# A graph layer on one core: VectorE's hand-written order changed, so that large additions from SBUF stand apart

## The chip, the core and the metric

One Trainium2 chip, one core of it. The metric is the device time of one launch, in microseconds. All data are fp32 at the kernel's border; x has 50,000 rows of 128, there are 25,000 edges.

## What is computed

The layer is a residual graph block. Every row of x is layer-normalised and cut at zero, the edges' attributes are summed per source node, a two-layer perceptron takes both, its result is normalised again, and both inputs are added back:

```python
h = maximum(layernorm(x), 0)                       # 50000 x 128
agg = segment_sum(edge_attr_128, src, 50000)       # 25000 edges, 128 wide
z = silu(concat([h, agg]) @ W1 + b1) @ W2 + b2     # 256 -> 256 -> 128
z = (z - mean(z)) * rsqrt(var(z) + 1e-5) * gamma + beta
out = x + (z + h)
```

## The kernel before, in words

The program is fully unrolled, and each engine's instructions stand in an order written out by hand, with semaphores between the engines. It has two stages. Up to about 125 us a first stage finds, for each of 392 tiles of 128 nodes, which edges belong to it and packs one edge per slot (`hot_tile`, `hot_slot`, `rank`; then `slot_edge` and `slot_node`). The change does not touch it, and only its end, the start of the second, is seen below.

The second stage runs over 49 blocks of 1,024 nodes (8 tiles of 128 each), and each block in two halves `c` of 4 tiles. The engines are several steps apart in it:

- SyncE loads X (512 KB a block, four blocks ahead) and stores R, the result, once both `result` operations of its block are done.
- POOL (GpSimd) fetches the edges' rows. For each tile it copies one column of `slot_edge` into `gather_rows` (line 418) and then issues one indirect DMA into G (line 430): 8 copies and 8 gathers a block, in turn. G has three buffers, so POOL can be up to three blocks ahead of TensorE.
- TensorE, per half: `turn_h` transposes H (line 595) into `za`; `sum_edges` (line 602) waits for the four gathers of that half and sums them there with the one-hot matrices HOT; `layer1` (lines 613, 614, 618) works on the half before; `layer2` (lines 626, 630) on the one before that. `turn_h` of a half needs `hi` and `lo` of the half before it to be taken out of `za`.
- ScalarE, per half: casts `za` to `hi` (lines 500, 502), squares of y for the second norm (515), `normalise` (493: H from X, with `shift` and `rstd`), and silu (508).
- VectorE, per block and in this order, in `step`: `split_low` of the second half (`lo<-za,hi`, line 870); a HOT matrix (861); `scale` of both halves (886: T from y, 4 operations each); `result` of both (896: R from T and R); `residual` (878: R from H and R); `split_low` of the next block's first half; then `powers` of a later block. `powers` is a chain of 13 small operations on 8 or 16 columns (lines 732 to 752) that gives both norms' `rstd` by Newton's steps. Each of the small ones waits for the one before it, and `link_small` puts another piece of work into that wait, by its place in the chain.

What VectorE's large operations read matters below. `R<-T,R`, `R<-H,R`, `R<-X,betas` and `HOT<-iota_node,slot_node` read two operands from SBUF, 512 columns each; there are two of each a block, eight in all. `lo<-za,hi` and `T<-y,rstd,gammas` read one from PSUM and one from SBUF; `stat<-X` (BN_STATS, line 697) reads one. In the text the eight are called **the eight additions**, though two of them compare.

Of the kernel before, what the change touches and what calls it, by code (L numbers as in the profile page):

```python
# [16 lines left out]
TILES = 8  # L17
# [72 lines left out]
def at_least(engine, semaphore, value):  # L90

    if value > 0:
        engine.wait_ge(semaphore, value)


def gnn_layer(nc, x, src, edge_attr, W1, b1, W2, b2, gamma, beta, out):
# [4 lines left out]
    NB = -(-nodes // BLOCK)  # L101
# [12 lines left out]
    with ExitStack() as ctx:  # L114
# [541 lines left out]
        def _(dve):  # L656
# [35 lines left out]
            def statistics(b, t):  # L692

                if t == 0:
                    dve.wait_ge(x_loaded[b.xj], b.x_lap(16, 16))
                    at_least(dve, powers_done, b.number(1, -1))
                done = nc.vector.bn_stats(stats[b.ring(2)][:, t, :], X[b.xj][:, t, :])  # L697
                if t == TILES - 1:
                    done.then_inc(bn_done, 1)

            SMALLS = 4 + 3 * NEWTON

            def powers(b):


# [3 lines left out]
                def link_small(instruction):  # L709

                    count[0] += 1
                    instruction.then_inc(small, 1)
                    place = count[0] - 1
                    if place == 0 and b.exists(NB) and not b.is_number(0):
                        one_hots(b, 0)
                    if 1 <= place <= TILES and b.plus(1).exists(NB):
                        statistics(b.plus(1), place - 1)
                    if b.plus(-2).exists(NB) and not b.is_number(0) and not b.is_number(1):
                        if place in (TILES + 1, TILES + 2):
                            x_plus_beta(b.plus(-2), place - TILES - 1)  # L720
                        if place == TILES + 3:
                            residual(b.plus(-2), 0)
                    dve.wait_ge(small, b.number(SMALLS, count[0]))

# [124 lines left out]
            def x_plus_beta(b, c):  # L849
                dve.wait_ge(x_loaded[b.xj], b.x_lap(16, 16))  # L850
                at_least(dve, stored[b.j], b.lap(16))
                s = slice(c * HALF, (c + 1) * HALF)
                nc.vector.tensor_tensor(out=R[b.j][:, s, :], in0=X[b.xj][:, s, :],
                                        in1=betas[:].unsqueeze(1).to_broadcast([P, HALF, D]),
                                        op=ALU.add).then_inc(xb_done, 1)
# [11 lines left out]
            def split_low(b, c):  # L867
                dve.wait_ge(hi_done, b.half(c, 1, 1))
                at_least(dve, pre_done, b.half(c, 2, -2))
                nc.vector.tensor_tensor(out=lo[c][:], in0=za[:], in1=hi[c][:].bitcast(F32),  # L870
                                        op=ALU.subtract).then_inc(lo_done, 1)

            def residual(b, c):

                dve.wait_ge(xb_done, b.half(c, 1, 1))
                dve.wait_ge(h0_done, b.half(c, 1, 1))
                s = slice(c * HALF, (c + 1) * HALF)
                nc.vector.tensor_tensor(out=R[b.j][:, s, :], in0=H0[b.j][:, s, :], in1=R[b.j][:, s, :],
                                        op=ALU.add).then_inc(r_done, 1)

            def scale(b, c):

                dve.wait_ge(powers_done, b.number(1, 1 + RING))
                for t in range(HALF):
                    n = TILES + c * HALF + t
                    done = nc.vector.scalar_tensor_tensor(  # L886
                        out=T[c][:, t, :], in0=y[2 * b.ring(2) + c][:, t * D:(t + 1) * D],
                        scalar=rstd[b.j][:, n:n + 1], in1=gammas[:], op0=ALU.mult, op1=ALU.mult)
                done.then_inc(t_done, 1)

            def result(b, c):

                dve.wait_ge(t_done, b.half(c, 1, 1))
                dve.wait_ge(r_done, b.half(c, 1, 1))
                s = slice(c * HALF, (c + 1) * HALF)
                nc.vector.tensor_tensor(out=R[b.j][:, s, :], in0=T[c][:], in1=R[b.j][:, s, :],
                                        op=ALU.add).then_inc(out_done, 1)
# [8 lines left out]
            def step(b):  # L906
                split_low(b, 1)
                if b.plus(1).exists(NB):
                    one_hots(b.plus(1), 1)
                if b.is_number(0):  # L910
                    slot_tables(FIRST_BLOCKS * TILES, NT)
                elif not b.is_number(1):
                    for c in range(2):
                        scale(b.plus(-2), c)
                    for c in range(2):
                        result(b.plus(-2), c)
                if not b.is_number(0):
                    residual(b.plus(-1), 1)
                if b.plus(1).exists(NB):
                    split_low(b.plus(1), 0)  # L920
                powers(b.plus(2))

            run_blocks(step)
# [32 lines left out]
```

## Time and profile before

| what | value |
|---|---|
| median of 3 runs | 801.94 us (800.46 to 802.87) |
| the profiled execution: its own time | 803.43 us |
| the profiled execution: its span | 801.9 us, 15882 instructions |
| TensorE busy, weight loads busy | 733.6 us (91%), 592.4 us (74%) |
| VectorE busy | 732.1 us (91%) |
| ScalarE busy | 587.0 us (73%) |
| POOL busy | 601.1 us (75%) |
| mean granted TensorE clock | 0.974 |

The page divides the span into 40 slices; from the sixth the second stage runs, and there TensorE and VectorE are busy over 90% of nearly every slice, and POOL about as much. Busy shares so high on three engines do not say which of them sets the pace; the chain of waits and the timelines do.

### The profile page before, as it was taken

The page shows a single profiled execution, that of the slowest core. Times are in us where ns is not written, and L with a number is a line of the kernel's source. Part 1 is how long each engine was busy: PE and PEld are TensorE (multiplying, and loading weights), DVE is VectorE, ACT ScalarE, POOL GpSimd, SP SyncE. Part 2 cuts the span into 40 slices and gives each one's busy share as a digit, 9 for nine tenths or more (in the row PEclk, how much of TensorE's full clock was granted, in tenths as well). Part 3 has the DMA queues.
Part 4 walks back from the last instruction along what each step waited for, and adds up shares of the span by engine and source line. Part 5 has one row for each costly group of instructions (what it writes and reads, how often), then busy time and mean ns, then how long its engine had stood idle before and what let it go on. Part 6 is the DMA issues. An engine that isn't in the chain of part 4 may idle for free.

```text
span 801.9 us, 15882 instructions
## 1 busy us (share of the span) xinstructions
PE 733.6 (91%) x4567; PEld 592.4 (74%) x4616; DVE 732.1 (91%) x2494; ACT 587.0 (73%) x1927; POOL 601.1 (75%) x831
## 2 busy tenths in 40 slices
PE   4999993989999999999999999999999999989990
PEld 1455542878888888888888888888888888878880
DVE  6999995879999999999999999999999999989994
ACT  4999982767777777777777777777777777757860
POOL 4600006889998999889989998999989998989920
PEclk9999995999999999999999999999999999999996
DMA  5000000122323333332323232323233332321211
GB/s 191 2 1 2 1 0 17 48 74 75 124 90 110 98 103 99 102 120 80 126 74 126 74 125 74 127 78 121 91 107 100 102 107 93 126 66 51 71 61 48
DMA packets 28159, 65.86 MB, mean 82 GB/s; under 512 B 8379, under 2 KB 9934, under 8 KB 28070
## 3 DMA queue, kind: packets, MB, share of 16 engines
q1 hardware_dynamic: 15526, 51.90, 18.6%
q0 software_dynamic: 12544, 12.93, 6.5%
q8 instruction: 37, 0.61, 0.3%
q14 instruction: 52, 0.43, 0.2%
HBM read 51.98 MB, written 25.60 MB: 97 GB/s over the span
## 4 chain that ended last, share of the span: by engine, by line
POOL 66%; ACT 10%; issue 8%; PE 8%; DVE 5%; DMA 1%; SPq 0%; POOLq 0%; DVEq 0%
POOL G L430 50%; POOL gather_rows L418 16%; ACT junk_rank L472 10%; PE y L630 2%; PE za L602 1%; PE pre L613 1%; PE pre L614 1%; DVE hot_tile L768 1%; PE pre L618 1%; DVE hot_slot L790 1%; DVE T L886 1%; DMA srci<-in_src_dram 1%; DMA G<-in_edge_attr_dram,gather_rows 1%; PE za L595 0%; DVE is_slot L781 0%
## 5 line engine op out<-in xcount | busy, mean ns | idle before, releaser
L430 POOL DMA_INDIRECT G<-in_edge_attr_dram,gather_rows x392 | 440.6, 1124 | 63.4 <-POOL gather_rows L418 48.2
L418 POOL COPY gather_rows<-slot_edge 128x1 uint32<-128x1 uint32 x392 | 138.5, 354 | 92.0 <-DVE slot_edge L842 89.6
L630 PE MATMUL y<-w2c,S 128*128 128x128 f32 x1568 | 190.9, 275 | 3.3
L630 PEld LDWEIGHTS y<-w2c,S 128*128 128x128 f32 x1568 | 191.5, 192 | 2.5
L493 ACT ACTIVATE H<-X,shift,rstd 128x128 f32<-128x128 f32 x392 | 162.4, 508 | 7.7 <-DVE shift L752 7.6
L613 PE MATMUL pre<-hi,w1h 128*128 128x512 f32 x392 | 164.8, 420 | 0.4 <-issue 0.4
L870 DVE TENSOR_TENSOR lo<-za,hi 128x1024 fp32r<-128x1024 f32 x98 | 119.8, 1222 | 46.5 <-ACT hi L502 42.3
L614 PE MATMUL pre<-hi,w1l 128*128 128x512 f32 x392 | 156.1, 398 | 0.0
L500 ACT CAST hi<-za 128x512 fp32r<-128x512 f32 x98 | 57.4, 586 | 123.5 <-PE za L595 113.6
L602 PE MATMUL za<-HOT,G 128*128 128x128 f32 x784 | 114.4, 290 | 18.4 <-issue 10.1
L508 ACT ACTIVATE S<-pre,b1c 128x512 f32<-128x512 f32 x196 | 125.3, 697 | 5.0 <-remote 2.1
L602 PEld LDWEIGHTS za<-HOT,G 128*128 128x128 f32 x784 | 97.1, 195 | 37.4 <-DMA G<-in_edge_attr_dram,gather_rows 31.5
L618 PE MATMUL pre<-lo,w1h 128*128 128x512 f32 x392 | 124.0, 397 | 0.0
L697 DVE BATCH_NORM_STATS2 stat<-X 128x6 f32<-128x128 f32 x392 | 109.0, 284 | 0.0
L515 ACT ACTIVATE junk_sq<-y 128x128 bf16<-128x128 f32 x392 | 103.7, 286 | 3.5 <-PE y L630 3.5
L886 DVE SCALAR_TENSOR_TENSOR T<-y,rstd,gammas 128x128 f32<-128x128 f32 x392 | 105.6, 341 | 0.0
L502 ACT CAST hi<-za 128x512 fp32r<-128x512 f32 x98 | 57.6, 588 | 42.4 <-PE za L602 25.0
L618 PEld LDWEIGHTS pre<-lo,w1h 128*128 128x128 f32 x392 | 74.4, 190 | 18.1
L613 PEld LDWEIGHTS pre<-hi,w1h 128*128 128x128 f32 x392 | 75.0, 191 | 14.3 <-issue 0.8
L515 ACT ACTIVATION_READ_ACCUMULATOR junk_sq<-y 128x1 f32 x392 | 85.0, 217 | 0.0
L614 PEld LDWEIGHTS pre<-hi,w1l 128*128 128x128 f32 x392 | 75.0, 191 | 13.4
L595 PE MATMUL za<-ident,H 128*128 128x128 f32 x392 | 59.8, 276 | 13.4 <-ACT H L493 9.0
(123 smaller groups left out, 1047.3 us busy)
## 6 DMA issues: line engine op xcount, KB each, us to landing
X<-in_x_dram SPq DMA_DIRECT2D x48, 512.0 KB
out_dram<-R SPq DMA_DIRECT2D x48, 512.0 KB
G<-in_edge_attr_dram,gather_rows POOLq DMA_INDIRECT x392
X<-in_x_dram SPq DMA_DIRECT2D x1, 424.0 KB
out_dram<-R SPq DMA_DIRECT2D x2, 212.0 KB
w1f<-in_L_gnn_W_dram SPq DMA_DIRECT2D x1, 256.0 KB, 3.3
w2f<-in_L_gnn_W_dram SPq DMA_DIRECT2D x1, 128.0 KB, 2.6
srci<-in_src_dram SPq DMA_DIRECT2D x1, 97.2 KB
```

What stands on the lines that cost most here:

```text
L418: nc.gpsimd.tensor_copy(gather_rows[b.xj][:, t:t + 1], slot_edge[:, bass.ds(b.number(TILES, t), 1)]).then_inc(row_named, 1)
L430: nc.gpsimd.indirect_dma_start(G[b.j][:, t, :], None, source, bass.IndirectOffsetOnAxis(ap=gather_rows[b.xj][:, t:t + 1], axis=0), bounds_ ...
L493: done = nc.scalar.activation(H0[b.j][:, t, :], X[b.xj][:, t, :], ACT.Relu, bias=shift[b.j][:, t:t + 1], scale=rstd[b.j][:, t:t + 1])
L508: nc.scalar.activation(S[c][:, m, :], pre[m][:], ACT.Silu, bias=b1c[:, m:m + 1]).then_inc(silu_done, 1)
L515: done = nc.scalar.activation(junk_sq[:, p, c * HALF + t, :], y[2 * p + c][:, t * D:(t + 1) * D], ACT.Square, scale=float(D) ** -0.5, accu ...
L602: done = nc.tensor.matmul(za[:, 1, t * P:(t + 1) * P], G[b.j][:, c * HALF + t, :], HOT[b.j][:, c * HALF + t, :], start=True, stop=True)
L613: nc.tensor.matmul(pre[m][:], w1h[:, k, cols], hi[c][:, k, :], start=(k == 0), stop=False)
L614: nc.tensor.matmul(pre[m][:], w1l[:, k, cols], hi[c][:, k, :], start=False, stop=False)
L618: done = nc.tensor.matmul(pre[m][:], w1h[:, k, cols], lo[c][:, k, :], start=False, stop=(k == 1))
L630: done = nc.tensor.matmul(place[:, t * D:(t + 1) * D], S[c][:, m, t * P:(t + 1) * P], w2c[:, m, :], start=False, stop=(t == HALF - 1 and m ...
L870: nc.vector.tensor_tensor(out=lo[c][:], in0=za[:], in1=hi[c][:].bitcast(F32), op=ALU.subtract).then_inc(lo_done, 1)
L886: done = nc.vector.scalar_tensor_tensor(out=T[c][:, t, :], in0=y[2 * b.ring(2) + c][:, t * D:(t + 1) * D], scalar=rstd[b.j][:, n:n + 1], i ...
```

## The change

VectorE's order in the second stage is written anew; no operation is added, removed or resized, and no other engine's order changes. In `powers` the fillers of the small chain are placed otherwise: BN_STATS at places 0, 2, 3, 5, 6, 8, 9 and 11, the HOT matrix at place 1, the two `x_plus_beta` at 4 and 7, the `residual` at 10 (before: HOT at 0, BN_STATS at 1 to 8, `x_plus_beta` at 9 and 10, `residual` at 11). In `step` the `residual` moves between the two `scale`, the first `result` follows the second `scale`, and `split_low` of the next half goes ahead of the second `result`.

```diff
+            STATISTICS_PLACES = (0, 2, 3, 5, 6, 8, 9, 11)
...
-                    if place == 0 and b.exists(NB) and not b.is_number(0):
+                    if place == 1 and b.exists(NB) and not b.is_number(0):
                         one_hots(b, 0)
-                    if 1 <= place <= TILES and b.plus(1).exists(NB):
-                        statistics(b.plus(1), place - 1)
-                    if b.plus(-2).exists(NB) and not b.is_number(0) and not b.is_number(1):
-                        if place in (TILES + 1, TILES + 2):
-                            x_plus_beta(b.plus(-2), place - TILES - 1)
-                        if place == TILES + 3:
+                    if place in STATISTICS_PLACES and b.plus(1).exists(NB):
+                        statistics(b.plus(1), STATISTICS_PLACES.index(place))
+                    if b.plus(-2).exists(NB):
+                        if place in (4, 7):
+                            x_plus_beta(b.plus(-2), (4, 7).index(place))
+                        if place == 10:
                             residual(b.plus(-2), 0)
...
-                elif not b.is_number(1):
-                    for c in range(2):
-                        scale(b.plus(-2), c)
-                    for c in range(2):
-                        result(b.plus(-2), c)
+                two_back = not b.is_number(0) and not b.is_number(1)
+                if two_back:
+                    scale(b.plus(-2), 0)
                 if not b.is_number(0):
                     residual(b.plus(-1), 1)
+                if two_back:
+                    scale(b.plus(-2), 1)
+                    result(b.plus(-2), 0)
                 if b.plus(1).exists(NB):
                     split_low(b.plus(1), 0)
+                if two_back:
+                    result(b.plus(-2), 1)
                 powers(b.plus(2))
```

VectorE, the first part of a step, before (T is the scaled result of the perceptron, R the sum that will be stored):

```order
L870 TENSOR_TENSOR lo1<-za,hi1 128x1024
L861 TENSOR_TENSOR HOT1<-iota_node,slot_node 128x512
L886 SCALAR_TENSOR_TENSOR T0<-y0,rstd1,gammas 128x128 x4
L886 SCALAR_TENSOR_TENSOR T1<-y1,rstd1,gammas 128x128 x4
L896 TENSOR_TENSOR R1<-T0,R1 128x512
L896 TENSOR_TENSOR R1<-T1,R1 128x512
L878 TENSOR_TENSOR R2<-H02,R2 128x512
L870 TENSOR_TENSOR lo0<-za,hi0 128x1024
L729 TENSOR_TENSOR msum<-stat0 128x8
```

The same part in the change; every line number behind the new table is higher by two:

```order
L872 TENSOR_TENSOR lo1<-za,hi1 128x1024
L863 TENSOR_TENSOR HOT1<-iota_node,slot_node 128x512
L888 SCALAR_TENSOR_TENSOR T0<-y0,rstd1,gammas 128x128 x4
L880 TENSOR_TENSOR R2<-H02,R2 128x512
L888 SCALAR_TENSOR_TENSOR T1<-y1,rstd1,gammas 128x128 x4
L898 TENSOR_TENSOR R1<-T0,R1 128x512
L872 TENSOR_TENSOR lo0<-za,hi0 128x1024
L898 TENSOR_TENSOR R1<-T1,R1 128x512
L731 TENSOR_TENSOR msum<-stat0 128x8
```

Three additions stood in a row; now a group of `T` or a `lo` stands between any two of them, and `lo0` has moved ahead of one.

VectorE, the end of `powers`, before (`guess_sq`, `guess_off` and `guess` are the small chain, 16 columns):

```order
L697 BN_STATS stat0<-X4 128x6
L750 SCALAR_TENSOR_TENSOR guess0<-guess_off,guess1 128x16
L853 TENSOR_TENSOR R1<-X1,betas 128x512
L747 SCALAR_TENSOR_TENSOR guess_sq<-guess0 128x16
L853 TENSOR_TENSOR R1<-X1,betas 128x512
L749 TENSOR_TENSOR guess_off<-guess_sq,var 128x16
L878 TENSOR_TENSOR R1<-H01,R1 128x512
L750 SCALAR_TENSOR_TENSOR rstd0<-guess_off,guess0 128x16
```

The same end in the change, from the second of the two `R<-X,betas`:

```order
L855 TENSOR_TENSOR R1<-X1,betas 128x512
L751 TENSOR_TENSOR guess_off<-guess_sq,var 128x16
L697 BN_STATS stat0<-X4 128x6
L752 SCALAR_TENSOR_TENSOR guess0<-guess_off,guess1 128x16
L697 BN_STATS stat0<-X4 128x6
L749 SCALAR_TENSOR_TENSOR guess_sq<-guess0 128x16
L880 TENSOR_TENSOR R1<-H01,R1 128x512
L751 TENSOR_TENSOR guess_off<-guess_sq,var 128x16
L697 BN_STATS stat0<-X4 128x6
L752 SCALAR_TENSOR_TENSOR rstd0<-guess_off,guess0 128x16
```

Between two additions there was one small operation; now there are three and two BN_STATS. The first `R<-X,betas` stands as far ahead of the second. A small operation of two SBUF operands still stands right before and right behind each of these additions.

## Rows read from the trace of the kernel before

**Rows 1.** The page: shares of the chain that ended last, by line
```profile
POOL G L430 50%; POOL gather_rows L418 16%; ACT junk_rank L472 10%; PE y L630 2%; PE za L602 1%; PE pre L613 1%; PE pre L614 1%; DVE hot_tile L768 1%; PE pre L618 1%; DVE hot_slot L790 1%; DVE T L886 1%; DMA srci<-in_src_dram 1%; DMA G<-in_edge_attr_dram,gather_rows 1%; PE za L595 0%; DVE is_slot L781 0%
```

**Rows 2.** Groups of POOL, 206 to 710 us: xcount | busy us, mean ns | idle before
```profile
L430 POOL DMA_INDIRECT G<-in_edge_attr_dram,gather_rows x307 | 341.8, 1113 | 48.6 <-POOL gather_rows L418 39.9 <-issue 8.7
L418 POOL COPY gather_rows<-slot_edge 128x1 uint32<-128x1 uint32 x307 | 112.0, 365 | 1.9
```

**Rows 3.** Lines L418 and L430, whole span: duration ns min/median/max
```profile
L418 POOL COPY gather_rows<-slot_edge x392: 185/199/1185, 123.6 to 765.1; 128x1 uint32<-128x1 uint32 x196
...
L430 POOL DMA_INDIRECT G<-in_edge_attr_dram,gather_rows x392: 997/1030/2731, 125.9 to 767.5; - x196
```

**Rows 4.** Timeline of TensorE: start us, length us, form, idle before
```profile
205.63 1.16 PE L602 MATMUL za<-HOT,G 128*128 128x128 f32 x8
...
710.13 1.16 PE L602 MATMUL za<-HOT,G 128*128 128x128 f32 x8
...
733.52 1.06 PE L602 MATMUL za<-HOT,G 128*128 128x128 f32 x8
...
739.67 1.06 PE L602 MATMUL za<-HOT,G 128*128 128x128 f32 x8
...
770.48 1.16 PE L602 MATMUL za<-HOT,G 128*128 128x128 f32 x8
```

**Rows 5.** Timeline of VectorE, parts of 421 to 444 us
```profile
421.30 1.28 DVE L896 TENSOR_TENSOR R<-T,R 128x512 f32<-128x512 f32 x2
422.50 0.69 DVE L878 TENSOR_TENSOR R<-H,R 128x512 f32<-128x512 f32 x1
...
430.58 1.22 DVE L870 TENSOR_TENSOR lo<-za,hi 128x1024 fp32r<-128x1024 f32 x1
431.72 0.68 DVE L861 TENSOR_TENSOR HOT<-iota_node,slot_node 128x512 f32<-128x512 f32 x1
432.32 2.15 DVE L886 SCALAR_TENSOR_TENSOR T<-y,rstd,gammas 128x128 f32<-128x128 f32 x8
434.39 1.28 DVE L896 TENSOR_TENSOR R<-T,R 128x512 f32<-128x512 f32 x2
...
436.97 1.22 DVE L870 TENSOR_TENSOR lo<-za,hi 128x1024 fp32r<-128x1024 f32 x1 [0.70 <-ACT hi L502]
...
439.85 0.16 DVE L747 SCALAR_TENSOR_TENSOR guess_sq<-guess 128x16 f32<-128x16 f32 x1
439.92 0.28 DVE L697 BATCH_NORM_STATS2 stat<-X 128x6 f32<-128x128 f32 x1
440.13 0.15 DVE L749 TENSOR_TENSOR guess_off<-guess_sq,var 128x16 f32<-128x16 f32 x1
...
443.66 1.22 DVE L870 TENSOR_TENSOR lo<-za,hi 128x1024 fp32r<-128x1024 f32 x1
```

**Rows 6.** Timeline of POOL, 420 to 424 us
```profile
420.54 0.20 POOL L418 COPY gather_rows<-slot_edge 128x1 uint32<-128x1 uint32 x1
420.89 1.03 POOL L430 DMA_INDIRECT G<-in_edge_attr_dram,gather_rows  x1 [0.15 <-issue]
421.93 0.69 POOL L418 COPY gather_rows<-slot_edge 128x1 uint32<-128x1 uint32 x1
422.78 1.30 POOL L430 DMA_INDIRECT G<-in_edge_attr_dram,gather_rows  x1 [0.16 <-POOL gather_rows L418]
```

**Rows 7.** Timeline of POOL and VectorE, 725 to 728 us
```profile
725.88 1.28 DVE L896 TENSOR_TENSOR R<-T,R 128x512 f32<-128x512 f32 x2
725.93 2.73 POOL L430 DMA_INDIRECT G<-in_edge_attr_dram,gather_rows  x1 [0.16 <-issue]
```

**Rows 8.** Chain of waits in order of time, near 714 us
```profile
714.23 5.26 DMA G<-in_edge_attr_dram,gather_rows
```

**Rows 9.** Timelines of ScalarE and TensorE, 431 to 435 us
```profile
431.43 1.66 ACT L493 ACTIVATE H<-X,shift,rstd 128x128 f32<-128x128 f32 x4
...
434.53 0.60 PE L595 MATMUL za<-ident,H 128*128 128x128 f32 x4
```

## The prediction

> **What bounds the kernel now.** I read the chain of waits first, because three engines look full. It runs through POOL's gathers for 50% of the span and through its copies for 16% [rows 1]: in the second stage POOL works without a pause and the rest follows. TensorE confirms it. Its `sum_edges` starts 77 halves apart at 205.63 and 710.13 us, so 6.55 us a half and 13.10 a block; later, once it is not waiting for gathers, the same work takes 6.15 us from 733.52 to 739.67, 12.30 a block [rows 4]. So 0.80 us a block is TensorE waiting for POOL.
>
> POOL is slow because of VectorE. A copy takes 0.199 us at the median and a gather 1.030, but the means from 206 to 710 us are 0.365 and 1.113 [rows 2, 3]. The excess is 0.166 + 0.083 = 0.249 us a tile, 1.99 a block of 8 tiles. The idle time is (48.6 + 1.9)/307 = 0.16 us a tile, its normal spacing before a gather. Unhindered, a tile costs 0.20 + 0.16 + 1.03 = 1.39 us and a block 11.11; 11.11 + 1.99 = 13.10, the pace seen.
>
> Where the excess arises is seen with two timelines side by side. Two `R<-T,R` start at 421.30 and 421.90 and `R<-H,R` at 422.50, 0.60 us each [rows 5]. The copy of 421.93, just behind the second one's start, ends at 422.62, 0.12 after that addition's end; the gather of 422.78 falls into the third and ends at 424.08, 0.98 after its end at 423.10, so 0.27 late [rows 6]. The copy of 420.54 takes 0.20: VectorE reaches its additions only at 421.30 [rows 5, 6]. So POOL needs a door that is shut while VectorE reads two SBUF operands. **The rule I use**: a copy that starts inside an addition (or up to about 0.07 before it) ends 0.12 after it; a gather that starts inside ends 0.98 after it.
>
> Does adjacency itself matter? The copy of 421.93 got through between two additions that touch. The gather of 725.93, 0.05 after the first of three, was kept out by all three: 725.88 + 3 x 0.60 + 0.98 = 728.66, its end [rows 7]. So the door can stay shut over a row of additions, but rarely did.
>
> **The change part by part.** Nothing is added or removed, on any engine or queue, so what VectorE executes costs 0. The order moves each addition; three things follow.
>
> *1. POOL's waits.* Take the first `lo` of the step as 0. From the spacings in [rows 5] (`lo` 1.14, an addition 0.60, four `T` 1.04, a BN_STATS 0.20, a small one 0.08) the additions now begin at 1.14 (HOT), 2.78, 4.42, then 6.16 (behind `lo0`), 7.3, 8.6, 9.8 and 11.05 (the last four inside `powers`), and the next step at about 12.3. Lay POOL's cycle (copy at 0, gather at 0.35, next copy at 1.39) beside it, beginning with a copy at 6.3 in the addition of 6.16 to 6.76:
> copy 6.3 held 0.43, gather 7.1 free; copy 8.1 and gather 8.4 free, between 7.9 and 8.6; copy 9.5 free; gather 9.8 meets an addition's start and is held 0.56; copy 11.4 held 0.2; gather 12.0, copy 13.0 and gather 13.4 free; copy 14.4 free; gather 14.7 free; copy 15.8 and gather 16.1 free; copy 17.2 held 0.04; gather 17.6 free, and the next copy is at 18.6, which is 6.3 again one step later. The waits sum to 1.23 us. If the gather of 9.8 wins its race, it is held 0.44 one addition later and the copies of the next step 0.11 and 0.25: again 1.23. POOL would need 11.11 + 1.23 = 12.34 a block.
> The reason in words: the additions used to stand in a row of three and, in `powers`, three with 0.08 between them, and a POOL instruction let in behind one fell into the next; now they are 1.1 to 1.7 us apart, close to POOL's own 1.39, and a released copy leads POOL through the gaps. Bounds: above all zero waits, 11.11, where TensorE decides; below, 8 additions at 0.43 or more, 14.6.
>
> *2. Who is next.* TensorE needs 12.30 [rows 4]. VectorE takes 443.66 - 430.58 = 13.08 with 0.70 idle before `lo0`, so 12.38 of its own [rows 5]. POOL at 12.34, TensorE at 12.30 and VectorE at 12.38 nearly tie; I take 12.38. Over the 38.5 blocks that POOL now paces this is 38.5 x (13.10 - 12.38) = 27.7 us less. The other blocks already ran at TensorE's pace; I add 0.4 us for VectorE there.
>
> *3. The late gather.* One gather issued at 714.23 landed only after 5.26 us [rows 8]. The nine halves from 710.13 to 770.48 took 60.35 us instead of 9 x 6.15 = 55.35 [rows 4]: 5.0 lost, since POOL had no lead. With POOL no longer the bound, it keeps whatever lead it has early on, G has three buffers, and such a landing is covered. I count the 5.0 as gained; if POOL's lead is used up, it stays.
>
> *4. `lo0` ahead of a result.* One 0.60 addition moves from before `lo0` to behind it. The stretch from `lo0` to the next `lo1` grows from 6.69 to 7.29 [rows 5] against halves of 6.15, so `lo1` and the `shift` right before it come up to 1.1 us after `hi`. Covers: ScalarE's `normalise` begins at 431.43, 0.85 after `lo1` at 430.58, and needs only the `shift` before it, so it slips by about 0.3; its H is ready at 433.09 and TensorE's transposes of it begin at 434.53, 1.44 later [rows 5, 9], of which halves shorter by 0.4 leave enough. `lo1`, ready at 431.8, has 2.7 to spare for them. Cost 0; without the cover, 0.3 us a block, 12 in all. The second `T` group and the second `result` come one addition later, and a store with them; that R buffer is needed again a block later: 0.
>
> **Sum.** 803.4 - 27.7 + 0.4 - 5.0 = 771.1 for an execution like the profiled one. That one lies 1.5 above the median of 801.9, so **770 us** against the median.
>
> **The rivals.**
> *A, the forecast* (0.60): 12.3 to 12.4 a block, 765 to 776.
> *B, POOL still paces, but less* (0.20): the walk above has close races (at 8.4, 9.8 and 13.4). Losing one and settling in another pattern leaves 1.4 to 1.8 of waiting, 12.5 to 12.9 a block: 38.5 x 0.2 to 0.6 = 8 to 23 us less, 779 to 794. For it: a difference of 0.05 us decides each race.
> *C, no change* (0.08): each of the eight additions still shuts the door for 0.60, and what counts is their total, 4.8 us a block before and after. POOL's cycle of 1.39 meeting an addition at any phase waits 0.42 on average where the next to come is a gather (0.35 of 1.39) and 0.17 where it is a copy, together 0.23: 8 x 0.23 = 1.9, nearly the 1.99 seen. Then 13.1 stays, 802. The Trainium skill, SBUF — State Buffer, section on SBUF's two separate sides, states this: a VectorE instruction with two SBUF inputs and a GpSimd instruction that reads SBUF exclude each other, each for its whole instruction, so adjacency alone should be free. By that rule the copy of 421.93 agrees and the gather of 725.93 does not. Against C speaks that phases are not random: POOL's waits repeat from block to block, since a wait ends on VectorE's beat.
> *D, slower* (0.12): with additions 1.2 to 1.3 apart, POOL may lock in just behind the start of each. Copies there wait 0.43 to 0.5 and gathers up to 0.56. Five such waits are 2.4 us, 13.5 a block: 38.5 x 0.4 = 15 more, 817. It decides from 2.0 us of waiting a block on. The last blocks speak for it a little: there, with TensorE at its own pace, one wait grew to 1.70 [rows 7].
>
> **How the numbers follow.** Faster by over 0.3% (about what a measurement of this kernel can tell) is A and B: 0.80. Same is C: 0.08. Slower is D: 0.12. The range for 8 in 10 holds A and nearly all of B, and 5 us below the forecast for smaller losses: 764 to 793.
>
> **What would show it.** In the changed profile POOL's mean copy should fall from 0.365 to about 0.29 and its mean gather from 1.113 to 1.10, together 1.2 to 1.3 us of excess a block; `sum_edges` should start 6.15 to 6.2 us apart; POOL's share of the chain should fall far below its 66%, TensorE and VectorE taking it; the wait of TensorE's weight loads for G should nearly vanish, and VectorE's wait before `lo0` shrink from 0.70 to below 0.2. If POOL's excess stays near 2.0, point 1 is wrong and C holds; if it falls to 1.2 while the blocks stay above 12.6, point 2 or 4 is.

## The result and the profile after

The changed kernel takes 768.83 us at the median of four runs (767.88 to 771.23), the kernel before 802.4 beside it; the ratio is 0.9589, 95% interval 0.9558 to 0.9619. It is 4.1% faster. The forecast was 770, and the profiled execution, for which the prediction's sum gave 771.1 before the last step to the median, took 771.23.

The page of the kernel after: spans and busy times, and the chain that ended last by engine and by line.

```profile
span 769.7 us, 15882 instructions
...
PE 717.4 (93%) x4567; PEld 590.0 (77%) x4616; DVE 733.0 (95%) x2494; ACT 586.2 (76%) x1927; POOL 563.7 (73%) x831
...
DVE 63%; issue 14%; ACT 10%; POOL 5%; PE 3%; DMA 2%; DVEq 0%; SPq 0%; POOLq 0%
DVE T L888 12%; ACT junk_rank L472 10%; DVE lo L872 8%; DVE HOT L863 7%; DVE R L855 7%; DVE stat L697 6%; POOL G L430 4%; DVE R L898 4%; DVE R L880 4%; DVE guess_sq L749 3%; DVE guess_off L751 2%; DVE guess L752 1%; POOL gather_rows L418 1%; DVE hot_tile L770 1%; DVE rstd L752 1%
```

POOL's 66% of the chain [rows 1] have become 5%, and the bulk of it now runs along VectorE's own instructions, line after line. VectorE's busy time is what it was, 733.0 against 732.1 us; it is the 32 us of span around it that have gone. A share of the chain tells where one chain ran, though, and not how much time an engine has to spare: see e7 below.

The groups of POOL of the kernel after, 206 to 710 us (columns as in [rows 2]):

```profile
L430 POOL DMA_INDIRECT G<-in_edge_attr_dram,gather_rows x325 | 357.8, 1101 | 51.9 <-POOL gather_rows L418 51.9
L418 POOL COPY gather_rows<-slot_edge 128x1 uint32<-128x1 uint32 x325 | 93.2, 287 | 2.0
```

In the same 504 us POOL now issues 325 gathers instead of 307. A gather is 0.071 us above its median of before, a copy 0.088: 0.159 a tile, 1.27 a block, where it was 1.99.

TensorE's timeline of the kernel after (start us, length us, form):

```profile
204.37 1.06 PE L602 MATMUL za<-HOT,G 128*128 128x128 f32 x8
...
682.39 1.06 PE L602 MATMUL za<-HOT,G 128*128 128x128 f32 x8
688.53 1.06 PE L602 MATMUL za<-HOT,G 128*128 128x128 f32 x8
694.78 1.06 PE L602 MATMUL za<-HOT,G 128*128 128x128 f32 x8
...
738.05 1.06 PE L602 MATMUL za<-HOT,G 128*128 128x128 f32 x8
```

The first two rows are the same halves, 77 apart, as the first two of [rows 4]. They give the account of the whole difference, in executions of 801.9 and 769.7 us of span:

| stretch | before | after | difference |
|---|---|---|---|
| up to `sum_edges` of half 11 | 205.63 | 204.37 | -1.26 |
| the next 77 halves | 504.50 | 478.02 | -26.48 |
| the last nine halves | 60.35 | 55.66 | -4.69 |
| from the last `sum_edges` to the end | 31.42 | 31.65 | +0.23 |
| sum | | | -32.2 |

A block takes 12.42 us instead of 13.10, and its two halves are unequal, 6.14 and 6.25 us in the rows above.

### The profile page after: what moved, and what is told of

Read it like the earlier page. It is cut to its first block, busy times and chain, and to the rows that moved or that the text cites. A ratio compares the mean times of both kernels' runs of the same rounds, so it can differ in the third digit from the quotient of the medians.

```text
span 769.7 us, 15882 instructions
## 1 busy us (share of the span) xinstructions
PE 717.4 (93%) x4567; PEld 590.0 (77%) x4616; DVE 733.0 (95%) x2494; ACT 586.2 (76%) x1927; POOL 563.7 (73%) x831
## 4 chain that ended last, share of the span: by engine, by line
DVE 63%; issue 14%; ACT 10%; POOL 5%; PE 3%; DMA 2%; DVEq 0%; SPq 0%; POOLq 0%
DVE T L888 12%; ACT junk_rank L472 10%; DVE lo L872 8%; DVE HOT L863 7%; DVE R L855 7%; DVE stat L697 6%; POOL G L430 4%; DVE R L898 4%; DVE R L880 4%; DVE guess_sq L749 3%; DVE guess_off L751 2%; DVE guess L752 1%; POOL gather_rows L418 1%; DVE hot_tile L770 1%; DVE rstd L752 1%
## 5 line engine op out<-in xcount | busy, mean ns | idle before, releaser
L430 POOL DMA_INDIRECT G<-in_edge_attr_dram,gather_rows x392 | 430.4, 1098 | 63.8 <-POOL gather_rows L418 62.2
L418 POOL COPY gather_rows<-slot_edge 128x1 uint32<-128x1 uint32 x392 | 111.3, 284 | 92.0 <-DVE slot_edge L844 89.6
L872 DVE TENSOR_TENSOR lo<-za,hi 128x1024 fp32r<-128x1024 f32 x98 | 119.3, 1218 | 13.3 <-ACT hi L502 13.2
L508 ACT ACTIVATE S<-pre,b1c 128x512 f32<-128x512 f32 x196 | 123.6, 684 | 1.8 <-PE pre L618 1.7
L602 PE MATMUL za<-HOT,G 128*128 128x128 f32 x784 | 106.9, 280 | 5.0 <-DMA G<-in_edge_attr_dram,gather_rows 5.0
L888 DVE SCALAR_TENSOR_TENSOR T<-y,rstd,gammas 128x128 f32<-128x128 f32 x392 | 109.6, 341 | 0.0
L614 PEld LDWEIGHTS pre<-hi,w1l 128*128 128x128 f32 x392 | 74.4, 190 | 13.3
L595 PE MATMUL za<-ident,H 128*128 128x128 f32 x392 | 62.0, 281 | 11.0 <-ACT H L493 9.0
```

The source lines that it names most:

```text
L430: nc.gpsimd.indirect_dma_start(G[b.j][:, t, :], None, source, bass.IndirectOffsetOnAxis(ap=gather_rows[b.xj][:, t:t + 1], axis=0), bounds_ ...
L508: nc.scalar.activation(S[c][:, m, :], pre[m][:], ACT.Silu, bias=b1c[:, m:m + 1]).then_inc(silu_done, 1)
L602: done = nc.tensor.matmul(za[:, 1, t * P:(t + 1) * P], G[b.j][:, c * HALF + t, :], HOT[b.j][:, c * HALF + t, :], start=True, stop=True)
L614: nc.tensor.matmul(pre[m][:], w1l[:, k, cols], hi[c][:, k, :], start=False, stop=False)
L888: done = nc.vector.scalar_tensor_tensor(out=T[c][:, t, :], in0=y[2 * b.ring(2) + c][:, t * D:(t + 1) * D], scalar=rstd[b.j][:, n:n + 1], i ...
```

## What the eight additions do to POOL now

VectorE's timeline of the kernel after, the additions and `lo` of one step:

```profile
424.07 1.21 DVE L872 TENSOR_TENSOR lo<-za,hi 128x1024 fp32r<-128x1024 f32 x1
425.20 0.67 DVE L898 TENSOR_TENSOR R<-T,R 128x512 f32<-128x512 f32 x1
426.34 0.68 DVE L863 TENSOR_TENSOR HOT<-iota_node,slot_node 128x512 f32<-128x512 f32 x1
427.64 0.68 DVE L855 TENSOR_TENSOR R<-X,betas 128x512 f32<-128x512 f32 x1
...
428.88 0.68 DVE L855 TENSOR_TENSOR R<-X,betas 128x512 f32<-128x512 f32 x1
...
430.23 0.68 DVE L880 TENSOR_TENSOR R<-H,R 128x512 f32<-128x512 f32 x1
...
436.53 1.21 DVE L872 TENSOR_TENSOR lo<-za,hi 128x1024 fp32r<-128x1024 f32 x1
```

POOL's timeline of the kernel after, the same microseconds:

```profile
423.87 0.32 POOL L418 COPY gather_rows<-slot_edge 128x1 uint32<-128x1 uint32 x1
...
425.38 0.58 POOL L418 COPY gather_rows<-slot_edge 128x1 uint32<-128x1 uint32 x1
...
428.53 0.20 POOL L418 COPY gather_rows<-slot_edge 128x1 uint32<-128x1 uint32 x1
428.89 1.61 POOL L430 DMA_INDIRECT G<-in_edge_attr_dram,gather_rows  x1 [0.16 <-POOL gather_rows L418]
430.51 0.46 POOL L418 COPY gather_rows<-slot_edge 128x1 uint32<-128x1 uint32 x1
```

These four are all that POOL waits for in a step. The walk in the prediction put them at the same additions: the copy in the `R<-T,R` behind `lo0` (0.43 forecast, 0.58 - 0.20 = 0.38 here), the gather that meets the start of the second `R<-X,betas` (0.56; 1.61 - 1.03 = 0.58), the copy at `R<-H,R` (0.2; 0.26) and the one at the next step's `R<-T,R` (0.04; 0.12). One block later the large ones stand at the same places: copies of 0.57 at 437.85 and 0.46 at 442.97, the gather of 1.61 at 441.36.

## The experiments

Their texts call the theory of the prediction's first point "phases": only where a POOL instruction's start falls decides what it waits. The rival is "adjacency": what costs is that additions touch.

### The two halves of the change

**e1_step_only** keeps the new `step` and has the old table in `powers`:

```diff
-                    if place in STATISTICS_PLACES and b.plus(1).exists(NB):
-                        statistics(b.plus(1), STATISTICS_PLACES.index(place))
+                    if 1 <= place <= TILES and b.plus(1).exists(NB):
+                        statistics(b.plus(1), place - 1)
...
-                        if place in (4, 7):
+                        if place in (TILES + 1, TILES + 2):
```

> Only the part of the change in `step` (residual between the two scales, lo0 ahead of the second result); `powers` keeps the fillers of before. Theory 1, phases: what counts is where POOL's cycle of 1.39 us meets the eight additions. Laid beside this order, POOL's copies and gathers run into about five of the eight, some 2.3 us of waiting a block, so 13.3 to 13.5 us a block and about 812 us: slower than the kernel before, although half of the adjacent additions are apart. Theory 2, adjacency: what counts is that additions no longer touch; the three in a row are apart now, those of `powers` not, so about half of the gain, 783 to 788. Theory 3, POOL's total wait is set by the total time of the additions: no change, 802.

Measured: 821.75 us (817.26 to 824.01), ratio 1.0243 [1.0195, 1.0291]. **Half of the change alone makes the kernel slower than it was**, though fewer additions touch than before. Its groups of POOL, 206 to 710 us:

```profile
L430 POOL DMA_INDIRECT G<-in_edge_attr_dram,gather_rows x297 | 339.0, 1141 | 47.3 <-POOL gather_rows L418 47.3
L418 POOL COPY gather_rows<-slot_edge 128x1 uint32<-128x1 uint32 x297 | 117.2, 395 | 1.6
```

The excess is 8 x (0.111 + 0.196) = 2.46 us a block, 11.11 + 2.46 = 13.57; `sum_edges` of successive blocks starts 13.52 apart on average. The walk had put it at 13.3 to 13.5 and the time at 812, so it had the sign and missed the size by 10 us. The mean is not a steady beat: TensorE mostly goes at 6.15 a half for four to six halves and then waits, as here:

```profile
422.17 1.06 PE L602 MATMUL za<-HOT,G 128*128 128x128 f32 x8
428.48 1.16 PE L602 MATMUL za<-HOT,G 128*128 128x128 f32 x8
437.53 1.59 PE L602 MATMUL za<-HOT,G 128*128 128x128 f32 x8 [2.65 <-DMA G<-in_edge_attr_dram,gather_rows]
```

POOL has no lead there, so TensorE waits for a gather that lands late, and behind such a wait its granted clock is lower too: 0.69 of full speed from 437.5 to 443 us. The prediction's fourth rival, 13.5 a block and 817 us, is nearly this state.

**e2_powers_only** keeps the new table and has the old `step`:

```diff
-                if two_back:
-                    scale(b.plus(-2), 0)
+                elif not b.is_number(1):
+                    for c in range(2):
+                        scale(b.plus(-2), c)
+                    for c in range(2):
+                        result(b.plus(-2), c)
                 if not b.is_number(0):
                     residual(b.plus(-1), 1)
-                if two_back:
-                    scale(b.plus(-2), 1)
-                    result(b.plus(-2), 0)
                 if b.plus(1).exists(NB):
                     split_low(b.plus(1), 0)
-                if two_back:
-                    result(b.plus(-2), 1)
```

> Only the part of the change in `powers`; `step` keeps the three additions in a row and lo0 behind them. Theory 1, phases: about 2.05 us of waiting a block, 13.1 us a block, 802 us, no gain from half of the change. Theory 2, adjacency: about half of the gain, 783 to 788. Theory 3: 802.

Measured: 796.59 us (793.76 to 797.36), 0.9929 [0.9903, 0.9954]; POOL paces with 66% of the chain. Its groups of POOL, 206 to 710 us:

```profile
L430 POOL DMA_INDIRECT G<-in_edge_attr_dram,gather_rows x310 | 364.2, 1175 | 49.0 <-POOL gather_rows L418 49.0
L418 POOL COPY gather_rows<-slot_edge 128x1 uint32<-128x1 uint32 x310 | 90.0, 290 | 1.9
```

8 x (0.145 + 0.091) = 1.89 a block, and 13.02 between blocks. The wait has moved from the copies to the gathers and hardly shrunk. The parts bring +2.4% and -0.7%; together they bring -4.1%. A cost for each addition, or for each pair that touches, would add up. This doesn't, so adjacency as a fixed price per pair falls; the phases theory had both signs nearly right (slower, no change) but neither size.

**e3_lo_last** undoes only the last move, of `lo0` ahead of the second `result`:

```diff
-                if b.plus(1).exists(NB):
-                    split_low(b.plus(1), 0)
                 if two_back:
                     result(b.plus(-2), 1)
+                if b.plus(1).exists(NB):
+                    split_low(b.plus(1), 0)
```

> The whole change but for lo0, which goes behind the second result again, so that two additions touch. Theory 1, phases: 1.7 to 2.1 us of waiting a block, 12.8 to 13.2 us a block, 790 to 804 us: most of the gain gone through one moved operation. Theory 2, adjacency: one touching pair of eight additions, most of the gain stays, 769 to 776. Theory 4, that an earlier lo frees TensorE and that this is the gain: 802, but then with POOL's waits near 1.35.

Measured: 783.39 us (781.18 to 786.84), 0.9761 [0.9731, 0.9792], between the two expectations. Groups of POOL, 206 to 710 us:

```profile
L430 POOL DMA_INDIRECT G<-in_edge_attr_dram,gather_rows x316 | 342.8, 1085 | 50.2 <-POOL gather_rows L418 50.2
L418 POOL COPY gather_rows<-slot_edge 128x1 uint32<-128x1 uint32 x316 | 110.2, 349 | 1.9
```

8 x (0.055 + 0.150) = 1.64 a block, 12.84 between blocks, POOL at 66% of the chain. Taking back one exchange, `lo0` 0.60 us later and a `result` 1.14 earlier, costs 14.6 of the 33.6 us gained. Neither theory had its size.

The traces of e2 and e3 show what both theories left out. POOL and VectorE of e2, then of e3:

```profile
415.31 1.28 DVE L898 TENSOR_TENSOR R<-T,R 128x512 f32<-128x512 f32 x2
415.33 2.78 POOL L430 DMA_INDIRECT G<-in_edge_attr_dram,gather_rows  x1 [0.16 <-POOL gather_rows L418]
416.51 0.69 DVE L880 TENSOR_TENSOR R<-H,R 128x512 f32<-128x512 f32 x1
```

```profile
426.25 1.28 DVE L898 TENSOR_TENSOR R<-T,R 128x512 f32<-128x512 f32 x2
426.55 1.02 POOL L418 COPY gather_rows<-slot_edge 128x1 uint32<-128x1 uint32 x1
```

The gather ends at 418.11, 1.00 us after the end of the third addition at 417.11; the copy ends at 427.57, 0.12 after the end of the second at 427.45. Both began in the first addition of a row of touching ones and were let in only behind the row. From 206 to 710 us that is the usual case: of the POOL instructions that begin in such a row ahead of its last addition, e2 keeps 37 out to the row's end and lets 2 in between; e3 keeps out 32 and lets in 7. In the kernel before there are 38, all of them copies that begin 0.02 to 0.04 us after the start of the second addition, and all are let in behind that one. What decides between the two cases no run shows. So touching additions do cost, but only where POOL's phase puts an instruction into the row: waits over more than one addition are some 1.5 of the 1.89 us a block in e2 and 0.7 of the 1.64 in e3, and in this window there are none in the kernel before, in e1 or in the kernel after. The rule of the prediction, out at the end of the addition in which it began, does not hold for those waits.

### POOL relieved

The rows of before offer another way: eight copies of one column, each with its own chance to meet an addition, could be one copy of eight columns. **e4_before_one_copy** does that to the kernel before, **e5_after_one_copy** to the kernel after:

```diff
-            def name_row(b, t):
+            def name_row(b):
...
-                nc.gpsimd.tensor_copy(gather_rows[b.xj][:, t:t + 1],
-                                      slot_edge[:, bass.ds(b.number(TILES, t), 1)]).then_inc(row_named, 1)
+                nc.gpsimd.tensor_copy(gather_rows[b.xj][:],
+                                      slot_edge[:, bass.ds(b.number(TILES), TILES)]).then_inc(row_named, 1)
...
-                    if t + 1 < TILES:
-                        name_row(b, t + 1)
-                    elif b.plus(1).exists(NB):
-                        name_row(b.plus(1), 0)
-                    at_least(pool, row_named, b.number(TILES, t + 1))
+                    if t + 1 == TILES and b.plus(1).exists(NB):
+                        name_row(b.plus(1))
+                    if t == 0:
+                        at_least(pool, row_named, b.number(1, 1))
```

> The kernel before, with one copy of 8 columns a block on POOL in place of 8 copies of one. POOL then needs about 8 x 1.19 + 0.36 = 9.9 us a block and the waits of the gathers alone. All theories that make POOL the bound of the kernel before: its pace falls to VectorE's or TensorE's, 12.3 to 12.4 us a block, 766 to 772 us, without any change of VectorE's order. If POOL is not the bound: 802.

> The changed order together with one copy of 8 columns a block on POOL. In the changed kernel VectorE sets the pace (12.43 us a block, no idle time), against 12.29 in the run of the kernel before with one copy, where TensorE does. Theory 1: VectorE's extra 0.14 is time for which it waits at POOL's copies and gathers, most of it in the small operations; with 7 of 8 copies gone VectorE falls to about 12.3 and the time to 760 to 764 us, like e4, so that VectorE's order is then worth nothing. Theory 2: the 0.14 belongs to the new order itself (its places for the fillers, lo1 late): VectorE stays at 12.4, 766 to 769 us, and the new order is slower than the old one once POOL is relieved.

Measured: 760.78 us (760.35 to 761.84), 0.9493 [0.9467, 0.9519], and 760.53 us (760.01 to 761.29), 0.9485 [0.9469, 0.9501]. **Both beat the change, and with POOL relieved the change is worth nothing**: the intervals overlap almost wholly. Every block takes 12.29 in both, which is TensorE's pace. The expectation for e4 was 766 to 772 and missed by 5 us: it took VectorE's 12.38 for VectorE's own need, and the same instructions in the same order fit into 12.29 once POOL's seven copies are gone. From the page of e4, the chain by engine:

```profile
PE 78%; ACT 11%; DVE 6%; issue 2%; DMA 1%; POOL 1%; SPq 0%; POOLq 0%; DVEq 0%
```

The groups of POOL of e4, 206 to 710 us:

```profile
L428 POOL DMA_INDIRECT G<-in_edge_attr_dram,gather_rows x329 | 403.7, 1227 | 94.5 <-issue 87.5 <-POOL gather_rows L417 6.7 <-PE za L600 0.3
L417 POOL COPY gather_rows<-slot_edge 128x8 uint32<-128x8 uint32 x41 | 8.2, 199 | 0.2
```

A copy of eight columns takes 0.199 us, the median of a copy of one [rows 3]. A gather takes 1.227, longer than in the kernel before with its 1.113, and yet the kernel is 5% faster. So a long POOL instruction by itself says nothing; see the last section.

The small operations of VectorE show the other side of the door. Groups of VectorE, 206 to 710 us, of the kernel before:

```profile
L750 DVE SCALAR_TENSOR_TENSOR guess<-guess_off,guess 128x16 f32<-128x16 f32 x76 | 11.8, 155 | 0.0
...
L750 DVE SCALAR_TENSOR_TENSOR rstd<-guess_off,guess 128x16 f32<-128x16 f32 x39 | 6.4, 163 | 0.0
```

Of the kernel after:

```profile
L752 DVE SCALAR_TENSOR_TENSOR guess<-guess_off,guess 128x16 f32<-128x16 f32 x81 | 15.2, 188 | 0.0
L752 DVE SCALAR_TENSOR_TENSOR rstd<-guess_off,guess 128x16 f32<-128x16 f32 x41 | 8.7, 212 | 0.0
```

Of e5:

```profile
L750 DVE SCALAR_TENSOR_TENSOR guess<-guess_off,guess 128x16 f32<-128x16 f32 x82 | 12.7, 155 | 0.0
...
L750 DVE SCALAR_TENSOR_TENSOR rstd<-guess_off,guess 128x16 f32<-128x16 f32 x41 | 6.4, 156 | 0.0
```

They too read two operands from SBUF. In the kernel after one `guess` of the two and the `rstd` are longer in every block, by 2 x 0.033 + 0.049 = 0.12 us together; in e5, with the same order on VectorE but other phases of POOL, they are not. VectorE pays at the door as well, and the 0.12 is about the difference between 12.42 and 12.29.

### Load added to POOL, and a surprise

**e6_before_pool_tick** and **e7_after_pool_tick** add one semaphore increment on POOL behind each gather:

```diff
+                    pool.sem_inc(pool_passed)
```

> The kernel before, with one more instruction of POOL's sequencer per gather (a count on a semaphore that nobody waits for), some 0.03 to 0.06 us each by the other sequencer gaps, so 0.25 to 0.5 us a block on the engine that is the bound. Theory 1, phases: POOL comes to the door later and waits less there; the wait falls from 1.99 to about 1.6, the pace stays at 13.1 us and the time within 4 us of before, 801 to 806. Theory 2, the waits are simply added to POOL's own time: 38.5 blocks times 0.25 to 0.5, so 812 to 821 us.

> The changed kernel with the same additional instruction per gather. Theory 1, phases: POOL is held at VectorE's beat, its excess of 1.35 us a block falls by what is added and the time stays, 768 to 771 us. If the added time is above 0.1 us a tile the fit is lost: 13.3 us a block, 800. Theory 2, added: since POOL has a lead of 5 us and never waits for TensorE, it falls behind by 0.25 to 0.5 us a block and becomes the bound after some 15 blocks: 775 to 785 us.

Measured: 801.27 us, 0.9992 [0.9982, 1.0002], and 767.93 us, 0.9579 [0.9562, 0.9597], against their common kernel before. The means of POOL are as without it (gather 1.110 and 1.099, copy 0.366 and 0.286), and the next copy still starts right at the gather's end. The increment added no time to POOL's cycle, so these two tell nothing of the theories. The page of e7 tells something else. Its chain by engine:

```profile
POOL 65%; ACT 11%; issue 9%; PE 6%; DVE 6%; DMA 1%; POOLq 1%; SPq 0%; DVEq 0%
```

That is 65% for POOL, where the kernel after has 5%, with 12.41 us a block against 12.42 and the same waits of POOL. In e7 POOL's lead is 2.1 to 3 us in most blocks (from the end of a block's last gather to its `sum_edges`), in the kernel after 6.4, and with the small one TensorE waits for G now and then, 4.4 us in all from 206 to 710 us. POOL and VectorE keep one beat in both; the lead decides on which of them the chain lands. So the 5% of the kernel after does not mean that its POOL has time to spare.

**e8_before_pool_work** and **e9_after_pool_work** put a spare one-column memset on POOL behind each half's gathers instead, **e11_after_half_pool_work** behind the first half's alone:

```diff
+        spare = sb("spare", [P, 1], F32)
...
+                nc.gpsimd.memset(spare[:], 0.0)
```

> The kernel before, with one memset of a spare column on POOL behind every half's gathers, 2 a block. It works on one column like the copies, so it should take POOL 0.1 to 0.2 us each, 0.2 to 0.4 us a block, on the engine that is the bound. Theory 1, phases: POOL is let through the door on VectorE's beat; what is added comes off its waits, which fall from 1.99 to 1.6 to 1.8 us a block, and the pace stays at 13.1: 800 to 806 us. Theory 2, added: 38.5 blocks times 0.2 to 0.4 more, 810 to 818 us.

> The changed kernel with the same 2 memsets a block. Theory 1, phases: POOL's waits fall from 1.35 to about 1.0 us a block, VectorE still paces at 12.4, 767 to 771 us. Theory 2, added: POOL falls behind VectorE by 0.2 to 0.4 us a block, uses up its lead of 5 us and paces in the second half of the blocks: 773 to 782 us.

> The kernel after, with one spare memset (115 ns) on POOL a block, behind the gathers of the first half only; with two a block the time was 826.6 instead of 768.8. Theory 1 (POOL's own load: what matters is the 0.1 to 0.2 us that POOL works more a block, which moves its waits): POOL needs 11.11 + 0.12 + some 1.3 = 12.5, a hair above VectorE's 12.43, so 768 to 775, and a step to 826 between 0.12 and 0.23 us of work would have to show as POOL in the chain. Theory 2 (the memsets bring on the stalls of ScalarE and VectorE that no recorded releaser ends, each of some us): half as many memsets bring half as many stalls, so about 790 to 800, with POOL absent from the chain and waiting for TensorE now and then.

Measured: e8 806.28 us (802.62 to 813.6), 1.0028 [0.9997, 1.0058]; e9 826.61 us (826.05 to 840.48), 1.027 [1.0216, 1.0324]; e11 804.05 us (800.74 to 805.66), 0.9999 [0.9979, 1.0018]. On the kernel before it does nothing that can be told apart, on the kernel after it costs 58 us, and half of it 35. Both theories missed e9, and e11 came out above what either gave. The profile of e9 shows no waiting for POOL: the gathers have become shorter, POOL waits for TensorE, and ScalarE and VectorE have stalls that end by nothing the profile names. Waits of e9, 206 to 710 us (engine, line, what it waited for: us, times, longest):

```profile
POOL gather_rows L419 <- PE za L604: 37.6, 28, 4.8
```

**e12_after_one_copy_pool_work** tells load from kind: the memsets are put into e5, where POOL doesn't pace:

```diff
+        spare = sb("spare", [P, 2 * RING], F32)
...
+                nc.gpsimd.memset(spare[:, 2 * b.j + c:2 * b.j + c + 1], 0.0)
```

> The kernel after with one 8-column copy a block on POOL (760.5 us by itself, POOL with 1.5 us to spare a block), and a spare memset of one column behind each half's gathers, as in the kernel that took 826.6. Theory 1 (the 826.6 comes of POOL's load or of the phase of its copies against VectorE): POOL has room for 0.23 us more, so 760 to 763. Theory 2 (a memset on POOL, wherever POOL stands, brings on the stalls of ScalarE and VectorE): 790 to 820, with the period of TensorE's sum_edges at 12.29 between the stalls.

Measured: 966.47 us (934.66 to 990.68), 27% over e5 at the median and 23% in the fastest execution, far above either expectation. The mean granted clock of the profiled one is 0.901, that of e5 0.980, so TensorE runs slower as well. From the page of e12, the group of the first `hi`:

```profile
L500 ACT CAST hi<-za 128x512 fp32r<-128x512 f32 x98 | 57.8, 590 | 187.4 <-remote 172.4
```

The timeline of e12 near 303 us, POOL, TensorE and ScalarE:

```profile
302.99 0.12 POOL L433 MEMSET spare<- 128x1 f32 x1
...
303.95 0.60 PE L595 MATMUL za<-ident,H 128*128 128x128 f32 x4
...
308.05 0.59 ACT L500 CAST hi<-za 128x512 fp32r<-128x512 f32 x1 [5.23 <-remote]
```

`hi` needs TensorE's transposes, which the record puts at 303.95 with 0.60 us, and starts 3.5 us after their end; a release came just before it, from a source the profile can't name. From 200 us on that happens in nearly every block, 38 times with 166.8 us in all. The stalls are not the effect of POOL's being far ahead: the first, of 5.6 us, comes in the third half, at whose start POOL has one gather in hand; it is the stalls that let POOL get ahead. **e13_after_one_copy_spare_copy** puts a one-column copy in the memset's place:

```diff
-                nc.gpsimd.memset(spare[:, 2 * b.j + c:2 * b.j + c + 1], 0.0)
+                nc.gpsimd.tensor_copy(spare[:, 2 * b.j + c:2 * b.j + c + 1],
+                                      slot_edge[:, bass.ds(b.number(TILES), 1)])
```

> The kernel after with one 8-column copy a block on POOL (760.5 us by itself), and behind each half's gathers, where a spare memset brought it to 966 us, a spare copy of one column instead, of the same kind as POOL's own copies (about 0.2 us, no semaphore, as the memset had none). Theory 1 (the kind of instruction: a POOL memset in this place brings on the stalls, in which ScalarE's hi waits 3 to 5 us for a release that the profile can't name): the copy brings none, POOL has room for 0.4 us more a block, so 760 to 765, and hi waits for TensorE alone. Theory 2 (any POOL instruction there without a semaphore, or the place in POOL's order ahead of its wait for a free G): the stalls come back, 850 or more.

Measured: 760.84 us (760.71 to 761.38), 0.9488 [0.9469, 0.9507]. From its page:

```profile
L501 ACT CAST hi<-za 128x512 fp32r<-128x512 f32 x98 | 57.4, 586 | 75.6 <-PE za L596 75.6
```

No such stall is left, and `hi` waits for TensorE alone. So the stalls come with the memset, not with any instruction in this place or with POOL's load; e8, e9 and e11 were therefore no measure of load. (The two differ in time as well as in kind, 0.12 us against 0.53 with its waits, and no run separates these.) By what path a memset on POOL delays the hand-over from TensorE to ScalarE stays open, and so does why the kernel before bears two of them a block with seven stalls of `hi`, and e12 has one a block. One wait of this sort, of 4.3 us, is in the kernel before too, with no memset near, so the memset is not its only cause.

## Why the prediction was right

**POOL's waits (point 1).** Forecast 1.23 us a block, measured 1.27; copies 0.29 forecast and 0.287 measured, gathers 1.10 and 1.101. The four waits of the walk are those of the trace, in their places. The race named as close, the gather of 9.8, is lost in each step shown. The rule that carried it, a copy ends 0.12 after the addition and a gather 0.98, holds within 0.04 us where no additions touch: the gather of 428.89 ends at 430.50, 1.02 after the addition's end at 429.48, and the copy of 430.51 ends 0.14 after that of its addition. The Trainium skill, SBUF — State Buffer, section "A bandwidth-pool intuition that's wrong (but worth ruling out)", says of a DMA issued from POOL beside a VectorE copy that it is "blocked until DVE-end + ~115 ns". The copies of this trace end 0.12 to 0.16 us after the addition and agree with that; a gather ends 0.98 to 1.02 after it, about its own 1.03 later. What rival C drew from the lock, that only the total of the additions counts, is refuted: the same eight additions cost POOL 1.27, 1.64, 1.89, 1.99 or 2.46 us a block by their places alone. Its premise, a lock for each single instruction, is not enough for the rows of touching additions in e2 and e3, where POOL is mostly kept out to the row's end.

**Who is next (point 2).** VectorE was named, at 12.38; it is VectorE, at 12.42, and its wait before `lo0` is gone (none from 206 to 710 us, 25.9 us before). That it has no idle time does not show it, since VectorE has none in e5 either, at TensorE's 12.29; what shows it is how long `normalise` waits for `shift`, 54.6 us in the same window against 8.2 in e5. The 12.38 was nearly right as a size and wrong as a kind: it was read as VectorE's own work, but e4 and e5 do the same work in 12.29. For the 12.42 the difference is about the 0.12 us by which VectorE's small operations are longer at the door; for the 12.38 no run takes it apart. The stretch brought 26.5 us, where 27.7 stood for it. That the sum met the profiled execution within 0.2 us (771.1 and 771.23) is partly luck: the 1.2 us that were missing here came in as 1.3 us gained before half 11, for which the sum had no gain.

**The late gather (point 3).** The last nine halves take 55.66 us; the sum had 55.35 + 0.4. Late landings have not gone. At 178 us, with no lead yet, one still cost some 4 us. After it POOL is four gathers ahead, and it stays there: POOL is through with the last gather of a block some 6.4 us before its `sum_edges` in nearly every block to the end, against some 1.5 before. TensorE's wait for G shows the same, 5.0 us of its page's group `za<-HOT,G` in all and none from 206 to 710 us. The 5.0 us that the prediction read off were not all waiting. TensorE stood for 3.0 us ahead of the `sum_edges` at 719.53, and from 719.8 to 723.2 its granted clock was 0.51 of full speed, the 1.2 GHz level, where it is 1.00 in the stretches around: the eight matmuls of that `sum_edges` took 1.82 us instead of 1.06. The same follows the wait of 2.5 us at 178 us in the kernel after (0.50 from 178.1 to 181.5). And the gain hangs on the lead: in e7, with its lead of 2.1 to 3 us, TensorE waits 1.9 us for a late gather near 692 us, and the last nine halves take 57.53 us instead of 55.66.

**`lo0` ahead (point 4).** This is the step that was nearly wrong. Waits of the kernel after, 206 to 710 us:

```profile
ACT H L493 <- DVE shift L754: 54.6, 41, 1.4
```

Timelines of ScalarE and TensorE of the kernel after:

```profile
431.58 1.65 ACT L493 ACTIVATE H<-X,shift,rstd 128x128 f32<-128x128 f32 x4 [1.42 <-DVE shift L754]
...
433.28 0.66 PE L595 MATMUL za<-ident,H 128*128 128x128 f32 x4
```

Once a block `normalise` waits 1.3 us for `shift`; H is ready at 433.23, and the transposes start at 433.28. The cover was 1.44 us [rows 9] and is used up. Cost 0 was right only because VectorE paces anyway: this is the place where its beat reaches TensorE, and why every second half is mostly 6.25 to 6.35 us long. The prediction let the cover shrink by 0.7 at most, from fixed distances. That was wrong in kind: if VectorE takes 12.4 a block and TensorE could do with 12.30, VectorE falls back by 0.1 a block against TensorE until some cover is gone and holds it, however long that cover is at first.

**The rivals.** B (POOL still paces) is what happens when one move is taken back (e3, 783), and D (slower) when the table is taken back (e1, 822): both were real states one edit away, so chances of 0.20 and 0.12 for them were not too much. That the walk hit 1.23 owes something to luck: the same walk missed e1 by 10 us, e2 by 5 and e3 by 7 or more. In e2 and e3 POOL falls into rows of touching additions, for which its rule is mostly wrong; the changed order has no such row, so there the rule was not put to that test.

## What to carry to other kernels

When a wait comes from two engines' beats meeting, neither a count of the conflicts nor an average over phases prices an order; lay the two cycles beside each other for a whole period, allow for a row of touching instructions to act as one long one, and expect parts of such a change to have other signs than the whole (+2.4% and -0.7% made -4.1%). Before tuning the phases look for the instruction to leave out: seven of eight 0.2 us copies fewer gave 5.1 to 5.2%, with either order. And a spare instruction put in to measure load has to be of a kind that is already there: a 0.12 us memset cost some 200 us in e12, a 0.2 us copy in its place nothing.

## What the runs showed that was not expected

POOL locks to VectorE's beat, also where it is not the bound. The held instructions of e4, e5 and e13 end at a fixed distance from an addition's end, as in the kernel before: gathers 0.95 to 0.98 us after it and copies 0.11 to 0.16, over 206 to 710 us. In e4, e5 and e13 it never has to wait for a free G to speak of (0.3 us from 206 to 710 us), it could run ahead, and yet its lead stays the same for over 400 us: 6.0, 12.5 and 6.7 us from the end of a block's last gather on POOL to its `sum_edges`. Its waits stretch to fill the block. The mean gather is 1.227, 1.191 and 1.125 us in three kernels of the same 12.29 us a block, and when two spare copies are added (e13), of 0.53 us each with their waits, the gathers and the idle time before them give back 0.9 us a block against e5. The excess of a locked engine's instructions is thus no measure of how much it has to spare. A lead that was won early, in a stall (the kernel after) or over a few blocks (e5, 1.2 to 1.3 us a block up to its 12.5), can be kept to the end; in e7 it shrank from 3.3 to 2.1 us within nine blocks.

A memset of 0.12 us on POOL brings stalls of 2 to 5 us and more on ScalarE (above), with the cause open.
